# Second attention: head 1's exponentials summed by one VectorE reduction over four tiles and the running total, per half of the columns

## The reference

```
# 16 heads of width 32, T = 2048 tokens
scores = einsum('bhtd,bhsd->bhts', Qf, Kf) / sqrt(32)
scores = where(causal, scores, finfo.min)
attn = softmax(scores, axis=-1)
out = einsum('bhts,bhsd->bhtd', attn, V)
return out.transpose(0, 2, 1, 3).reshape(B, T, C) @ Wp
```

## Time and profile before

| | us |
|---|---|
| runs shown | 2710.2, 2735.0, 2773.57 |
| median | 2735.0 |
| profiled execution, time | 2692.58 |
| profiled execution, span of its core | 2690.8 |
| busy in that span: PE | 2366.4 |
| busy: DVE | 1757.9 |
| busy: ACT | 1247.4 |
| busy: POOL | 512.0 |

### The profile page before, as it was taken

The page is one execution under the profiler, slowest core; times in us unless marked ns, Lnnn a source line. Parts: engine busy times, 40 slices in busy tenths (PEclk is TensorE's granted clock), DMA queues, the critical chain, the costliest instruction groups (busy, mean ns, idle before and its releaser), DMA issues. The chain is left out here.

```text
span 2690.8 us, 41814 instructions
## 1 busy us (share of the span) xinstructions
PE 2366.4 (88%) x16222; PEld 1471.9 (55%) x16222; DVE 1757.9 (65%) x2057; ACT 1247.4 (46%) x2357; POOL 512.0 (19%) x447
## 2 busy tenths in 40 slices
PE   4959999949999999999999479969969999999947
PEld 2758888824444454444443457758845555555515
DVE  3645444546888887888880343422259999999954
ACT  2422222203777876877876122212215565556631
POOL 1110000010000000000000002220026776667650
PEclk8979999955999997999995789989979999999978
DMA  3771000061121120220000420015561222220024
GB/s 128 235 230 47 32 32 31 0 79 21 29 45 31 29 45 19 41 39 18 10 9 4 143 63 0 1 41 116 194 142 47 59 65 65 65 63 10 10 65 143
DMA packets 121389, 164.66 MB, mean 61 GB/s; under 512 B 60848, under 2 KB 66608, under 8 KB 115824
## 3 DMA queue, kind: packets, MB, share of 16 engines
q1 hardware_dynamic: 117744, 149.52, 22.8%
q10 hardware_dynamic: 3456, 12.58, 1.4%
HBM read 114.19 MB, written 47.71 MB: 60 GB/s over the span
## 5 line engine op out<-in xcount | busy, mean ns | idle before, releaser
L615 ACT ACTIVATE a_ex<-a_ps_s 128x512 f32<-128x512 f32 (+3 forms) x1280 | 620.2, 532 | 293.9 <-PE a_ps_s L670 217.8
L768 DVE TENSOR_REDUCE a_mx_part<-a_ps 128x2 f32<-128x1024 f32 (+3 forms) x576 | 584.8, 1042 | 133.4 <-PE a_ps L635 131.2
L1040 ACT ACTIVATE a_ex<-a_ps_s 128x512 f32<-128x512 f32 (+3 forms) x640 | 318.2, 532 | 282.6 <-PE a_ps_s L1101 159.6
L635 PE MATMUL a_ps<-a_k,a_q 48*128 48x512 f32 (+3 forms) x1152 | 366.1, 439 | 43.8 <-DMA a_q<-q 29.5
L670 PE MATMUL a_ps_s<-a_q,a_k 50*128 50x512 f32 (+3 forms) x1152 | 400.9, 436 | 0.6 <-DMA a_q<-m 0.3
L713 PE MATMUL a_ps_o<-a_ex,a_v 128*32 128x256 f32 (+1 forms) x5120 | 379.4, 380 | 5.9 <-ACT a_o L603 5.1
L1015 POOL TENSOR_TENSOR a_acc<-a_acc,a_ex 128x512 f32<-128x512 f32 (+3 forms) x288 | 352.2, 1223 | 95.6 <-ACT a_ex L1040 74.7
L1165 DVE TENSOR_REDUCE a_mx_part<-a_ps 128x2 f32<-128x1024 f32 (+2 forms) x320 | 336.0, 1053 | 31.5 <-PE a_ps L1067 22.8
L670 PEld LDWEIGHTS a_ps_s<-a_q,a_k 50*128 50x128 f32 x1152 | 184.2, 196 | 216.7 <-ACT a_ex L615 167.9
L1668 POOL TENSOR_TENSOR gc_z<-gc_state,gc_qg 128x512 f32<-128x512 f32 x16 | 26.3, 1642 | 1193.9 <-DVE gc_qg L1656 1193.9
L1064 PE MATMUL a_ps<-a_k,a_q 96*128 96x512 f32 (+3 forms) x640 | 211.2, 396 | 43.9 <-DMA a_q<-q 23.0
(11 more groups left out here) (200 smaller groups left out, 3812.7 us busy)
## 6 DMA issues: line engine op xcount, KB each, us to landing
a_q<-q SPq DMA_DIRECT2D x48, 256.0 KB, 5.4
a_k<-k SPq DMA_DIRECT2D x24, 512.0 KB, 5.0
a_q<-q SPq DMA_DIRECT2D x24, 512.0 KB, 6.8
q<-p_oh SPq DMA_DIRECT2D x32, 256.0 KB, 2.5
q<-p_ol SPq DMA_DIRECT2D x32, 256.0 KB, 2.8
w_o<-o SPq DMA_DIRECT2D x8, 1024.0 KB
w_z<-z SPq DMA_DIRECT2D x32, 256.0 KB
a_k<-k SPq DMA_DIRECT2D x48, 128.0 KB, 3.4
```

Of the source, the lines that this page charges most:

```text
L615: act.activation(ex[unit % NE][:, h % 2, off:CH], ps_s[n % 3][:, off:CH], ACT.Exp, scale=SCALE)\
L635: mm = pe.matmul(ps_1[m % 2][:, e, 0:w], q_st[s][r0:r0 + KC, slot_h, i * P:(i + 1) * P], k_st[s][r0:r0 + KC, h % KH, kc * CH:kc * CH + w], ...
L768: dve.tensor_reduce(mx_part[:, 2 * p:2 * p + 2, i, kc], bank[:, :, 0:w], AX.X, ALU.max).then_inc(taken1, 1)
L1040: act.activation(ex[s % NE][:, h, off:CH], ps_s[n % 3][:, off:CH], ACT.Exp, scale=SCALE)\
```

## The change

The eight tiles of exponentials and two running totals for head 1 now lie in one array of ten places, `ex[:, place]`: totals in places 0 and 5 (only head 1's half of these is used), tiles of four steps each in places 1 to 4 and 6 to 9. For the open steps VectorE no longer adds tile by tile. For each four tiles it issues two TENSOR_REDUCE instructions, one for each half of the columns. Each adds, for 256 columns, four tiles and the running total beside them (for the first four tiles of a chunk the tiles alone), and writes the new total into the other total's place. It reads with the tiles as the innermost dimension, so that consecutive elements lie in different places, 4096 bytes apart. The reductions stand 5 and 6 steps after the first of the four steps, behind that step's maximum. The diagonal tiles are added one by one as before, two steps behind; the first of them reads the total from the place where the last reduction left it.

ACT's wait for head 1 is now for the instruction that reads the tile last (`READ`), and so is PE's before `sums`. The flipped maxima lie in PSUM partitions 64 to 71 rather than 0 to 7, and the two parts that DVE takes are kept in partitions 64 to 71 of `z_sb`. GpSimd's sums for head 0 are the same, at other addresses.

```diff
+    TOTAL = [0, NE // 2 + 1]
...
+    ADDS = []
+    for s, (g, c, t) in enumerate(STEP_LIST):
+        if t >= TPC * c:
+            ADDS.append((s + 2, s, None))
+        elif t % TPC == 0:
+            ADDS += [(s + TPC + 1 + half, s, half) for half in range(2)]
+    ADDS.sort(key=lambda a: a[0:2])
+    READ = {}
+    for n, (_, s, half) in enumerate(ADDS):
+        for tile in range(s, s + 1 if half is None else s + TPC):
+            READ[tile] = n + 1
+
+    def place(s):
+
+        return s % NE + 1 + (s % NE >= NE // 2)
...
-        ex = [sb(f"ex{i}", [P, HG, CH]) for i in range(NE)]
-        acc = [[sb(f"acc{i}_{n}", [P, CH]) for n in range(HG)] for i in range(2)]
+        ex = sb("ex", [P, NE + 2, HG, CH])
+        acc = [[sb(f"acc{i}_0", [P, CH])[:, :], ex[:, TOTAL[i], 0, :]] for i in range(2)]
...
-                        act.wait_ge(added1, s - NE + 1)
+                        act.wait_ge(added1, READ[s - NE])
...
-                pe.wait_ge(added1, s + 1)
+                pe.wait_ge(added1, READ[s])
...
-                bank = ps_1[m % 2][0:ROWS_F, 0, 0:P]
+                bank = ps_1[m % 2][OR:OR + ROWS_F, 0, 0:P]
...
+            def add_tiles(n, s, half):
 
                 g, c, t = STEP_LIST[s]
...
+                cols = slice(half * CH // 2, (half + 1) * CH // 2)
+                lo, hi = place(s) - (t > 0), place(s) + TPC
+                dve.wait_ge(exp_done, (s + TPC) * HG)
+                dve.wait_ge(added1, n)
+                dve.tensor_reduce(ex[:, TOTAL[1 - s // TPC % 2], 1, cols], ex[:, lo:hi, 1, cols].rearrange("p n k -> p k n"), AX.X, ALU.add)\
+                    .then_inc(added1, 1)
...
-                if 0 <= s - 2 < len(STEP_LIST):
-                    add_ex(s - 2)
+                for n, (at, first, half) in enumerate(ADDS):
+                    if at == s and half is None:
+                        add_tile(n, first)
+                    elif at == s:
+                        add_tiles(n, first, half)
```

More of the change, by code:

```diff
@@ L873, in attention_two @@
         o_sb = [sb(f"o{i}", [OR, CH]) for i in range(2)]
-        z_sb = [sb(f"z_sb{i}", [OR, CH]) for i in range(2)]
+        z_sb = [sb(f"z_sb{i}", [P, CH]) for i in range(2)]
         mx_part = sb("mx_part", [P, HG, QT, NCH])
         mx = [sb(f"mx{i}", [P, HG, TPC]) for i in range(2)]
-        rows = [[sb(f"rows{i}_{s}", [ROWS_F, P], F32R) for s in range(2)] for i in range(2)]
+        rows = [[z_sb[i][OR:OR + ROWS_F, part * P:(part + 1) * P].bitcast(F32R) for part in range(2)] for i in range(2)]
         z = [sb(f"z{i}", [P, ZN]) for i in range(NZ)]
@@ L926, in put_rows @@
                 for part in range(2):
-                    sp.dma_start(m_d[f, part], rows[b][part][:, :].bitcast(F32)).then_inc(rows_out[b], 16)
+                    sp.dma_start(m_d[f, part], rows[b][part].bitcast(F32)).then_inc(rows_out[b], 16)
                 sp.wait_ge(rows_out[b], 32 * (f // 2 + 1))
@@ L1006, in _ @@
                 j, off = g * NCH + c, first_col(c, t)
-                total, tile = acc[j % 2][0], ex[s % NE][:, 0, off:CH]
+                total, tile = acc[j % 2][0], ex[:, place(s), 0, off:CH]
                 pool.wait_ge(exp_done, s * HG + 1)
@@ L1074, in flip @@
                 pe.wait_ge(taken1, m - 1)
[L1075 removed]
+                pe.matmul(ps_1[m % 2][OR:OR + ROWS_F, 0, 0:P], mx[f % 2][:, :, :].rearrange("p h i -> p (h i)"),
                           neg_ident[:, :], start=True, stop=True).then_inc(scores1, 1)
@@ L1191, in take_sums, with add_tile @@
                     dve.wait_ge(z_stored[j % 2], 16 * HG * (j // 2))
-                dve.tensor_copy(z_sb[j % 2][:, :], ps_1[m % 2][0:OR, 0, :]).then_inc(taken1, 1)
-            def add_ex(s):
+                dve.tensor_copy(z_sb[j % 2][0:OR, :], ps_1[m % 2][0:OR, 0, :]).then_inc(taken1, 1)
+            def add_tile(n, s):
                 g, c, t = STEP_LIST[s]
                 j, off = g * NCH + c, first_col(c, t)
-                total, tile = acc[j % 2][1], ex[s % NE][:, 1, off:CH]
+                total, tile = acc[j % 2][1], ex[:, place(s), 1, off:CH]
                 dve.wait_ge(exp_done, (s + 1) * HG)
-                if t == 0 and j >= 2:
+                if n > 0:
+                    dve.wait_ge(added1, n)
+                if t == TPC * c and j >= 2:
                     dve.wait_ge(scores1, SUMS_ENTRY[j - 2] + 1)
@@ L1203, in add_ex @@
                     dve.tensor_copy(total[:, :], tile).then_inc(added1, 1)
-                    return
-                dve.wait_ge(added1, s)
-                dve.tensor_tensor(total[:, off:CH], total[:, off:CH], tile, ALU.add).then_inc(added1, 1)
+                else:
+                    before = ex[:, TOTAL[s // TPC % 2], 1, :] if t == TPC * c else total[:, off:CH]
+                    dve.tensor_tensor(total[:, off:CH], before, tile, ALU.add).then_inc(added1, 1)
+            def add_tiles(n, s, half):
+                g, c, t = STEP_LIST[s]
+                cols = slice(half * CH // 2, (half + 1) * CH // 2)
+                lo, hi = place(s) - (t > 0), place(s) + TPC
+                dve.wait_ge(exp_done, (s + TPC) * HG)
+                dve.wait_ge(added1, n)
+                dve.tensor_reduce(ex[:, TOTAL[1 - s // TPC % 2], 1, cols], ex[:, lo:hi, 1, cols].rearrange("p n k -> p k n"), AX.X, ALU.add)\
+                    .then_inc(added1, 1)
             def invert(g, c):
```

8 lines of the change are left out of this document (4 added, 4 removed).

## The result

The changed kernel takes 2856.4 us (median of 4, 2846.24 to 2909.16) beside 2722.6 for the kernel before (median of 4): 5.2% slower, ratio 1.052 with an interval of 1.046 to 1.058. The prediction's range ended at 2810. The runs of one kernel spread with PE's granted clock (the kernel before, 12 runs on one chip: 2670 us at 0.932 to 2809 us at 0.872), and every ratio here compares only the fast runs of both kernels, those within 1.5% of the kernel's fastest.

The account below looks back on a forecast made before the run. DVE was taken to set the second attention's pace. Instructions +18 us and idleness +10 us on the profiled 2692.6 gave 2720, ratio 1.010; on the runs' median of 2735.0 that is 2763 us, range 2685 to 2810.

Parts of the forecast that it names:

- What bounds the kernel: Second attention: DVE, busy 72.2 of 73 us a group, sets the pace; PE needs about 64 us and has slack.
- The prediction's own sign of being wrong: Reductions outside 1.35 to 1.87 ns an element, or a group moving by something other than DVE's sum.
- What is removed and added: DVE, per group: 21.2 us of additions and copies go, 23.4 us of reductions come at 1.63 ns an element; +18 us.
- The middle: Price of a reduction's element on DVE: 1.63 ns, taken between ends of 1.04 and 2.2 ns.
- The port: DVE's reductions beside POOL's additions: counted as unstretched; stretching by 0.36 us each would cost 35 us more.
- Uneven work: Starts of chunks 1 to 3: DVE idle up to 2.4 us a group, 19 us in all; half, 10 us, added.
- The granted clock: PE in the second attention: full granted clock read in the earlier profile; no term for a change in the sum.
- Rival (c), the ring: ACT's wait for sums isn't covered, up to 0.6 us at 48 places: 29 us more, 2792 us; chance 0.08.
- Rival (b): DVE's reductions: a hop costs as much as the scan's element, 2.2 ns; +93 us, ratio 1.035, 2829 us; chance 0.14.

Follow-up runs that it names:

- e10_even_work: Kernel before, with an extra reduction of 192 neighbouring elements ahead of each open tile's addition; fastest run 2779.6 us, 3.5% above the kernel before's four fastest.
- e8_before_fill: Kernel before, with PE issuing a head 1 product four times more ahead of the maximum's product in certain slots, 48 a group; ratio 1.022.
- e11_quarters: Changed kernel, with four reductions of 128 columns in slots 4 to 7 instead of two of 256, diagonal additions and sums shifted; fastest run 2812.4 us.
- e7_rows64: Kernel before, with only the flipped maxima and the two parts that DVE takes moved to partitions 64 to 71; ratio 1.009.
- e2_late_adds: Kernel before, with its old additions of head 1's open tiles done two in slot 5 and two in slot 6; ratio 1.015.
- e4_fill: Changed kernel, with PE issuing a head 1 product four times more ahead of the maximum's product where it waits behind a reduction; ratio 1.048.
- e1_dense: Changed kernel, with the same reductions in the same places reading elements that lie side by side, head 1's sums not right; ratio 1.025.
- e3_early: Changed kernel, with the reductions one step earlier, in slots 4 and 5, and a chunk's sums one step earlier; ratio 1.057.

## Why the prediction was wrong, point by point

**What bounds the kernel: half right.** DVE had 0.7 us of idle time in a group and more work on it lengthens the group, as e10_even_work shows. But the prediction gave PE 64 of 73 us, put together from start-to-start times at their best, and concluded that PE had room. e8_before_fill measures it: 11.3 us of PE work more lengthen a group by 8.1. Both engines are within a few per cent of being the bound, and there is little to even out one with the other. The prediction's own sign of being wrong was that "a group moves by something other than DVE's sum": DVE's sum rose by 6.5 us, the group by 19.

**What is removed and added: right, and the price close.** 1.75 ns an element against 1.63 between its ends of 1.04 and 2.2. The middle was a choice and not a measurement, so that it came close is partly luck. The Trainium skill's page "Vector Engine (DVE) Microarchitecture Reference", section "Measured stream behaviour on trn2", has 1.73 ns a column for one source that hops at every element. The traces agree within 3% (1.75 here, 1.77 by e11_quarters' (1287 - 1061) / 128), and the full-rate exception that it names doesn't extend to this reduction. DVE's busy time in a group rose by 6.4 us, not by 2.2. Of the 4.2 between them the reductions' own durations, 12 x 2.20 less the forecast's 23.4 + 12 x 0.08, are 2.0, the partitions of `take_rows` 0.5 (e7_rows64). The 1.7 left are about what is lost in overlap: the durations of DVE's instructions in such a group add up to 81.6 us before and 85.1 after, 8.1 and 5.3 above the busy times, and 12 instructions less, at 0.08 each, explain 1.0 of these 2.8. The forecast let every instruction overlap with the one in front, and one that starts behind a wait can't.

**The port: right.** The reduction doesn't stretch: side by side it took the 1478 and 1212 ns that rows without such a neighbour had given. POOL's additions went to 1286 ns and its busy time in a group from 51.3 to 47.4 us, but no group waited for POOL.

**Uneven work: the first step that failed, by its size.** "Together 2.4 us a group, 19 us in all, if nothing carries over; 0 if DVE comes in late enough. I add half, 10 us." The place was right: the trace shows DVE idle at the starts of chunks and at the sums. The size was not. With the old additions in the new places (e2_late_adds) idle time at a full clock is 6.6 us a group instead of 0.7, with the dense reductions 5.7, and the waits that make it up stand where the prediction looked, at the starts of chunks 1 to 3. The bound of 2.4 came from comparing four-slot sums and giving PE its best times, and it left out the waits for the chunk's sums (30 us in the changed kernel).

**The granted clock: the second step that failed, and the larger; it stood in the sum at nothing.** The prediction read "a full granted clock for PE" in the earlier trace rows and took it as given for the changed kernel as well. The groups of one kernel at several clocks give its price: 2.7 us for 0.04 in e4_fill, 2.4 in e1_dense, 2.6 in the kernel before, so some 0.65 us of a group for each 0.01. At that rate the changed kernel's groups of 91.8 and 95.9 us would be 84.6 and 85.5 at a full clock; by the difference between these two, 0.8 for each 0.01, they would be 83. Both are estimates from slopes, not seen: no group of it ran at a full clock.

**The account.** A group grew from some 75 to 94 us (the means of the six whole groups inside). 6.5 is DVE's busy time, measured. At a full clock of 83 to 85 us its idle time would be 3 to 5 instead of 0.7, so 2.5 to 4.5 is unevenness, by estimate. The remaining 8 to 10 are the clock. Over eight groups 52 us, 20 to 35, and 65 to 80, together some 150 where the span shows 154. The forecast had 18, 10 and 0. The three aren't separate causes: without the hop (e1_dense) most of the clock's loss goes too, its groups run at 0.94 to 1.00.

**Rival (c), the ring,** had the loudest witness in the profile after, 100 us of ACT waiting for the reductions, and a price of 29 us. e3_early takes 98 of the 100 us away and the kernel is no faster. **Rival (b)** named the right sign and something near the right size for a wrong reason: the price of the hop stayed below its threshold of 1.87 ns.

## What to carry to other kernels

Where two engines are coupled by two buffers and both are over 90% busy, the sum of work is only the first term: the same additions, later and two to a slot, cost 4.6 us of 74 with no instruction made dearer (e2_late_adds), because DVE stood in the slots left empty and was busy without a gap elsewhere. Ask then what the waits do to TensorE's granted clock; here letting it fall cost 8 to 10 us a group by estimate, the work that made it fall 6.5. And a new wait that tops the list needn't be worth anything: take it away before believing it.

## What the hardware showed that I had not expected

A PE wait of 1.8 us was followed by a stretch at 1.2 GHz in which PE was busy all the time and each product took 0.42 us from start to start instead of 0.235; all eight stretches at the lower clock in three groups of the changed kernel began during or right behind a wait of 1.8 to 2.9 us, and four of twelve such waits had none behind them. A reduction whose neighbours lie 4096 bytes apart in SBUF costs 1.75 to 1.78 ns an element, in runs of four and of five alike, against 1.04 side by side. Moving a copy from DVE to POOL made DVE's remaining two-input additions dearer, 1031 to 1132 ns, 2.4 us a group, more than the four copies took (2.0).
